# A two-layer block with a temporal conditioner: another order of the pieces on every engine, one of seven trace sums on VectorE, output rows normalised by ScalarE

## The reference, cut to what matters

```python
ctx = causal_ema(x, tau_ctx)                                    # a scan over the 512 tokens
wg = sigmoid(concat([x, ctx]) @ Wg.T + bg);  gated = x * wg
h1 = gelu(x @ Wn1.T + bn1);  mod = 0.5 + sigmoid(h1 @ Wn2.T + bn2)      # 8 values per token
traces = [causal_ema(gated * mod[:, d:d+1], tau[d]) for d in range(8)]
temporal = sum_d(softmax(blend)[d] * traces[d])
gate = sigmoid(temporal @ Wtemp.T + btemp)
soma = gelu(x @ Wsoma.T + bsoma)
out = (soma * gate) @ Wout.T
z = (out - mean(out)) / sqrt(var(out) + 1e-5) * gamma + beta
# then: router logits of z, the 8 largest of 64, their softmax weights; a shared expert on z;
# the 64 routed experts; x = x + routed + shared
```

## Time and profile before

| | before |
|---|---|
| median of 3 runs | 1252.2 us (1246.92 to 1252.47) |
| profiled execution: time, span | 1251.99 us, 1250.2 us |
| PE busy | 976.5 us (78%) |
| DVE busy | 742.4 us (59%) |
| POOL busy | 665.0 us (53%) |
| ACT busy | 455.0 us (36%) |
| mean granted TensorE clock | 0.880 of full speed |

### The profile page before, as it was taken

How to read it: one execution, slowest core, us unless ns; L and a number is a source line. 1 busy time by engine, 2 the same in 40 slices (tenths; PEclk the granted TensorE clock), 3 DMA queues, 4 the chain that set the end, 5 groups by cost and what they waited for, 6 DMA issues and landing times.

```text
span 1250.2 us, 15128 instructions
## 1 busy us (share of the span) xinstructions
PE 976.5 (78%) x4616; PEld 698.3 (56%) x4616; DVE 742.4 (59%) x1547; ACT 455.0 (36%) x811; POOL 665.0 (53%) x474
## 2 busy tenths in 40 slices
PE   5894079999999999875657778678657698888880
PEld 3673069998998999842224344344344365555550
DVE  1444656666665766416566666767774677666730
ACT  1221144635546445424343544444421032222230
POOL 1110224545535545238787586776872167777771
PEclk9765579999999999886878888898878799999995
DMA  2355714444444333232112231321311689998967
GB/s 65 114 164 186 270 44 104 87 92 109 88 113 84 88 72 52 51 101 76 44 68 73 88 118 56 105 89 69 124 55 39 225 212 250 257 253 242 259 105 147
DMA packets 90450, 151.22 MB, mean 121 GB/s; under 512 B 15816, under 2 KB 72848, under 8 KB 87248
## 3 DMA queue, kind: packets, MB, share of 16 engines
q1 hardware_dynamic: 55184, 95.46, 23.4%
q0 software_dynamic: 25104, 39.86, 17.4%
q10 hardware_dynamic: 10096, 15.10, 3.6%
HBM read 115.37 MB, written 43.42 MB: 127 GB/s over the span
## 4 chain that ended last, share of the span: by engine, by line
PE 47%; POOL 12%; issue 10%; DVE 10%; DMA 8%; POOLq 4%; DVEq 3%; ACT 2%; ACTq 0%
PE bank L1497 14%; PE bank L1482 13%; DMA out<-ys,slots 5%; POOL acc L604 5%; PE bank L1509 5%; PE bank L1598 4%; POOLq L603 3%; DMA odd_rows<-ys,slots 2%; POOL xg L650 2%; DVE body L1150 2%; POOL odd_rows L657 2%; POOL out L657 2%; PE bank L1404 2%; PE bank L1581 2%; PE bank L1467 1%
## 5 line engine op out<-in xcount | busy, mean ns | idle before, releaser
L801 ACT ACTIVATE h_raw<-bank,b 128x512 f32<-128x512 f32 x128 | 88.1, 688 | 168.8 <-PE bank L1482 166.5
L1150 DVE TENSOR_TENSOR_SCAN body<-bank,body 128x512 f32<-128x512 f32 x112 | 129.7, 1207 | 30.1 <-POOL acc L604 27.2
L1497 PE MATMUL bank<-w_hi,h_hi 128*128 128x256 f32 x512 | 144.6, 282 | 0.1
L1105 DVE TENSOR_TENSOR h_lo<-h_raw,h_hi 128x512 fp32r<-128x512 f32 x128 | 87.2, 692 | 94.3 <-ACT h_hi L805 94.3
L1497 PE MATMUL bank<-w_lo,h_hi 128*128 128x256 f32 x512 | 142.4, 278 | 0.0
L1497 PE MATMUL bank<-w_hi,h_lo 128*128 128x256 f32 x512 | 142.3, 278 | 0.0
L604 POOL TENSOR_TENSOR acc<-acc,body 128x1024 f32<-128x1024 f32 x56 | 132.3, 2363 | 12.8 <-issue 11.0
L578 POOL DMA_INDIRECT x_rows<-ob,put x64 | 110.5, 1727 | 27.7 <-issue 14.6
L1482 PE MATMUL bank<-ex_hi,w_hi 128*128 128x512 f32 x256 | 100.6, 393 | 4.9 <-issue 4.9
L1482 PE MATMUL bank<-ex_hi,w_lo 128*128 128x512 f32 x256 | 101.6, 397 | 0.0
L1482 PE MATMUL bank<-ex_lo,w_hi 128*128 128x512 f32 x256 | 101.2, 395 | 0.0
(11 more groups left out here) (229 smaller groups left out, 2191.0 us busy)
## 6 DMA issues: line engine op xcount, KB each, us to landing
body<-in_mwp SPq DMA_DIRECT2D x46, 512.0 KB, 4.4
head<-in_mwp SPq DMA_DIRECT2D x18, 512.0 KB
w1s<-in_fW SPq DMA_DIRECT2D x8, 1024.0 KB, 4.8
w2s<-in_fW SPq DMA_DIRECT2D x8, 1024.0 KB, 5.3
md<-m_rows SPq DMA_DIRECT2D x8, 1024.0 KB, 4.8
body<-m_rows SPq DMA_DIRECT2D x8, 1024.0 KB, 5.6
z_rows<-zrow SPq DMA_DIRECT2D x8, 640.0 KB, 3.2
xt<-in_x SPq DMA_DIRECT2D x8, 512.0 KB
```

The costliest lines, as they stand in the source:

```text
L801: A.activation(h1_raw[f % 4][:, :], bank[:, 2 + f % 4, :], ACT.Gelu_apprx_tanh, bias=b1_0[:, bass.ds(e, 1), f]).then_inc(b_h, 1)
L1105: V.tensor_tensor(h1_lo[:, f, :], h1_raw[f % 4][:, :], h1_hi[:, f, :].bitcast(F32), ALU.subtract).then_inc(b_lo, 1)
L1150: o = V.tensor_tensor_scan(dst[:, c, :], decay[:, d:d + 1].to_broadcast([P, S]), drive[(D * b + d) % DRIVES][:, c, :], 0.0, ALU.mult, ALU.add)
L1497: o = T.matmul(rows4(6)[:, j, :], x[:, f, rows], w[q][:, f * H:(f + 1) * H], start=(f == 0 and n == 0), stop=(f == FT0 - 1 and n == 2))
```

## The change

Every engine gets a new order of the same pieces, with loops over b written out. POOL, DVE and ACT of step b become (PE and SP in the diff):

- POOL: rstd_of(b-2), drive(b-1,7), add(b-1,5), drive(b,0), drive(b,1), add(b-1,6), add(b-1,7), drive(b,2), add(b,1), drive(b,3), drive(b,4), add(b,2), add(b,3), drive(b,5), drive(b,6).
- DVE: scan 0, scan 1, shared_b(b-2), ctx_scan(b+1), pick(b-2), scan 2, gate_soma(b-1), scan 3, shared_a(b-2), route_weights(b-2), scan 4, stats(b-1), add(b,4), scan 5, gate_in(b+1), scan 6, finish(b-2), scan 7.
- ACT: z_out(b-2), soma_out(b), weighted(b,2), x1T_out(b+1), shared_b_out(b-2), weighted(b,3), h1_out(b+1), gate_out(b-1), weighted(b,4), weighted(b,5), shared_out(b-2), exponentials(b-2), weighted(b,6), t8_out(b+1), weighted(b,7), wg_out(b+1), normalise(b-1), weighted(b+1,0), weighted(b+1,1).

The sum of trace 4 is made by DVE, the other six stay on POOL. The rows are normalised by ACT as rstd times out plus a shift, and POOL's `rstd_of` makes that shift with two more instructions of 128x4. The steps run from b = -1, and the last share from b = B + 1.

```diff
             def rstd_of(q):
                 pool.wait_ge(c_mv, level(q))
                 pool.wait_ge(c_no, level(q - 1))
-                settle(pool, tally)
                 G.tensor_scalar(veps1[:, :], mv1[:, :, 1], 4 * EPS, None, ALU.add)
+                G.tensor_scalar(shift1[:, :], mv1[:, :, 0], -1.0, None, ALU.mult)
                 pool.drain()
-                G.tensor_tensor(rstd1[:, :], veps1[:, :], mhalf[:, :], ALU.pow).then_inc(c_rs, 1)
+                G.tensor_tensor(rstd1[:, :], veps1[:, :], mhalf[:, :], ALU.pow)
+                pool.drain()
+                G.tensor_tensor(shift1[:, :], shift1[:, :], rstd1[:, :], ALU.mult).then_inc(c_rs, 1)
...
+            def normalise(q):                                  # ACT
+                act.wait_ge(c_rs, level(q))
+                act.wait_ge(c_zst, level(q - 1, 16))
+                act.wait_ge(c_zm, level(q - 1))
+                for j in range(TT):
+                    o = A.activation(zrow[:, j, 0:H], rows4(0)[:, j, :], ACT.Identity, bias=shift1[:, j:j + 1],
+                                     scale=rstd1[:, j:j + 1])
+                o.then_inc(c_no, 1)
...
+            def add_trace(b, d):                               # DVE
+                dve.wait_ge(c_scan, level(D * b + d))
+                if d > 1:
+                    dve.wait_ge(c_add, added(b, d - 1))
+                dve.drain()
+                V.tensor_tensor(acc[b % 2][:, :, :], acc[b % 2][:, :, :], trace[((D - 1) * b + d - 1) % TRACES], ALU.add).then_inc(c_add, 1)
...
             def route_weights(q):
                 dve.wait_ge(c_ex, level(q))
+                dve.wait_ge(c_zst, level(q - 1, 16))
...
             # SP, step b
-                if share:
-                    q = b - 2
-                    sp.wait_ge(c_fin, level(q - 1))
-                    sp.dma_start(xr[:, :, :], ...).then_inc(c_xr, 16)
-                    sp.wait_ge(c_zr, level(q))
-                    sp.dma_start(z_rows[...], zrow[:, :, :]).then_inc(c_zst, 16)
-                if front:
-                    m_load(b + 1, 0)
-                if share:
-                    sp.wait_ge(c_fin, level(q))
-                    sp.dma_start(out[...], ost[:, :, :]).then_inc(c_ost, 16)
-                if front:
-                    m_load(b + 1, 1)
+                if on(b - 2):
+                    row_in(b - 2)
                 if b == B:
                     sp.wait_ge(c_add, added(B - 1, D - 1))
                     for e in range(HEADS, RING):
                         e_load(e)
+                if ahead(b + 1):
+                    m_load(b + 1, 0)
+                if on(b - 2):
+                    z_store(b - 2)
+                if ahead(b + 1):
+                    m_load(b + 1, 1)
+                if on(b - 2):
+                    row_store(b - 2)
...
             # PE, step b
-                for d in range(D):
-                    if d == 0 and front:
-                        h1_in(b + 1)
-                    if d == 1 and share:
-                        shared_a_in(b - 2)
-                    if d == 1 and gate:
-                        temp_in(b - 1, 1 - p, front)
-                    if d == 2 and front:
-                        t8_in(b + 1)
-                    if d == 3 and gate:
-                        out_in(b - 1)
-                    if d == 3 and front:
-                        wg_in(b + 1, 0)
-                    if d == 4 and front:
-                        wg_in(b + 1, 1)
-                    if d == 4 and share:
-                        down_in(b - 2, gate, front)
-                    if d == 6 and front:
-                        soma_in(b + 1)
-                    if d == 6 and gate:
-                        z_in(b - 1)
-                    if d == 7 and gate:
-                        logits_in(b - 1)
-                    if d == 7 and load:
-                        x1T_in(b + 2, h + 1, p)
-                    if d == 7 and gate:
-                        shared_b_in(b - 1, front)
+                if ahead(b + 1):
+                    x1T_in(b + 1)
+                if on(b - 2):
+                    shared_b_in(b - 2)
+                if on(b - 2):
+                    logits_in(b - 2)
+                if ahead(b + 1):
+                    h1_in(b + 1)
+                if on(b - 1):
+                    temp_in(b - 1)
+                if on(b - 2):
+                    shared_a_in(b - 2)
+                if ahead(b + 1):
+                    t8_in(b + 1)
+                if on(b - 1):
+                    out_in(b - 1)
+                if ahead(b + 1):
+                    wg_in(b + 1)
+                if on(b - 2):
+                    down_in(b - 2)
+                if on(b - 1):
+                    z_in(b - 1)
+                if ahead(b + 1):
+                    soma_in(b + 1)
```

More of the change, by code:

```diff
@@ L350, in ffn, with on, ahead, conditioning @@
             group(E0 // 2 - 1, True)
[L352 to L358, removed]
+        def on(n):
+            return 0 <= n < B
+        def ahead(n):
+            return 0 < n < B
         def added(b, d):
             return level((D - 1) * b + d - 1)
-        def conditioning(eng, first, step):
+        def conditioning(first, step):
             first()
[L370 to L378, removed]
+            for b in range(-1, B + 2):
+                step(b)
         @block.sync
@@ L616, in _, with step @@
             ffn(pool, b_group)
-            def step(h, p, load, front, middle, gate, share):
-                b = 2 * h + p
-                for d in range(D):
[L621 to L633, removed]
+            def step(b):
+                if on(b - 2):
+                    rstd_of(b - 2)
+                if on(b - 1):
+                    drive_of(b - 1, 7)
+                if on(b - 1):
+                    add_trace(b - 1, 5)
+                if on(b):
+                    drive_of(b, 0)
+                if on(b):
+                    drive_of(b, 1)
+                if on(b - 1):
+                    add_trace(b - 1, 6)
+                if on(b - 1):
+                    add_trace(b - 1, 7)
+                if on(b):
+                    drive_of(b, 2)
+                if on(b):
+                    add_trace(b, 1)
+                if on(b):
+                    drive_of(b, 3)
+                if on(b):
+                    drive_of(b, 4)
+                if on(b):
+                    add_trace(b, 2)
+                if on(b):
+                    add_trace(b, 3)
+                if on(b):
+                    drive_of(b, 5)
+                if on(b):
+                    drive_of(b, 6)
+                if b == B:
+                    pool.wait_ge(c_som, level(B - 1))
+                    pool.drain()
+                    for r in range(RING):
+                        o = G.memset(wdb[r][0:P - FR, :], 0.0)
+                    o.then_inc(e_pad, 1)
@@ L917, in front_only @@
                 h1_out(0)
-                t8_out(0, 0)
+                t8_out(0)
                 wg_out(0)
-                soma_out(0, 0)
-                weighted(0, 0, 0)
-                weighted(0, 0, 1)
-                x1T_out(1)
-            conditioning(act, front_only, step)
+                soma_out(0)
+            conditioning(front_only, step)
             def silu(e):
@@ L1301, in last_share, with step @@
                 dve.drain()
-            def step(h, p, load, front, middle, gate, share):
-                b = 2 * h + p
-                if isinstance(b, int) and b == B + 1:
+            def step(b):
+                if b == B + 1:
                     dve.drain()
@@ L1687, in row_0 @@
                     t8_in(0)
[L1688 to L1689 removed]
+                    wg_in(0)
                 else:
```

269 lines of the change are left out of this document (152 added, 117 removed).

## The result

The changed kernel takes 1166.3 us (median of 4 runs, 1161.8 to 1167.2); the kernel before took 1251.7 beside it. The ratio is 0.932, with a 95% interval of 0.928 to 0.935. The forecast was 1176, with 1159 to 1204 as its range. The profiled execution took 1165.94 us, its span 1164.2.

A forecast was written before the change was run, and what follows sets the result against it. A ring of waits, not work, was taken to set the 50.9 us step. Five new steps of 39.5, limited by DVE (34.6 + 4.7), with first steps and tail, gain 76 us: span 1174.2 plus 1.8 is 1176 us, range 1159 to 1204.

The forecast's parts named there:

- What bounds it: Conditioning's 50.9 us middle step: a ring of waits; an older sequence's share delays the gate, blocking ACT, starving POOL 14.5 us.
- The step, 39.5: A middle conditioning step in the new order takes 39.5 us, with DVE as its limit; five such steps.
- the step is shorter than I think: Rival: DVE's waits come out smaller, POOL's 37.1 us limits the step, 12 us less, 1164; chance 0.12.
- the term of DVE: DVE per step: 34.6 us of work plus 4.7 for four waits on POOL (bounds 0 and 9.4), 39.3.
- The lock's price on POOL: POOL, held up by DVE instructions with two SBUF inputs, pays 1.1 us for the sum, 0.2 for each other.
- The first two steps: From drive(0,0) at 558.5, drive(1,0) comes at 589 and drive(2,0) at 626.5 us.
- `normalise` on ACT: ACT normalises the rows in four PSUM reads of 0.38, 1.5 us a step, covered by 2 us of slack.
- The tail: After the last sum: normalise(7) starts 20 us behind it instead of 20.8, then 24.7 us unchanged to the first gather.
- Tripping: Rival: nearly full POOL and DVE wait for each other, step 44 us, total 1200; chance 0.24, store's landings included.
- The wait of `normalise` for the store: Rival: z_store(b-2), behind m_load, lands late, 3 us a step, 15 us, 1191; counted within tripping's 0.24.
- PE at its lower clock: Rival: PE's matmuls run mostly at 1.2 GHz, PE needs 54.7 us a step, eating the gain; all low 1321; chance 0.05.
- Changes nothing: Rival: in the new order the ring through gate_out only closes elsewhere, 1252; chance 0.04.

The follow-up runs named there:

- order_only_early: Changed kernel with trace 4's sum back on POOL and normalise back on DVE, between scan 5 and gate_in, with the old rstd_of: 1179.7 us, ratio 0.944.
- normalise_on_dve_early: Changed kernel with normalise back on DVE, between scan 5 and gate_in, and the old rstd_of: 1177.5 us, ratio 0.940.
- pow_only_store_first: Changed kernel with rstd_of's two small preparations made by DVE behind stats, and z_store issued ahead of the experts' weights: 1165.3 us, ratio 0.932.
- more_dve: Changed kernel with one more 128x512 scan on DVE in each step, into a tile nothing reads: 1163.4 us, ratio 0.931.
- normalise_on_dve: Changed kernel with normalise back on DVE, between finish and the last scan, and the old rstd_of: 1193.3 us, ratio 0.955.
- moves_only: Kernel before, in its old order, with trace 4's sum moved to DVE and normalise to ACT: 1256.6 us, ratio 1.006.
- sum4_on_pool: Changed kernel with trace 4's sum put back on POOL, behind drive(b,6): 1177.1 us, ratio 0.944.

## Why the prediction was right, point by point

**What bounds it: half right.** That waits and not work set the step, that POOL starves for `gb`, and that the new order frees it, the changed kernel and order_only_early show. That one link, the share ahead of the gate, is the cause, they don't: exchanging that pair alone gave 0.4%, and 48.7 of POOL's 52.3 us of waits stayed. The prediction read the ring's last wait and took it for the whole ring; with the pair exchanged `temp_in` waits for the last sum instead, and the share's output on ACT still stands between the gate and `weighted`. It forecast the changed kernel rightly because the new order opens all links at once, and because the step was laid out engine by engine and not got by taking one wait off. Which exchanges of the new order are needed wasn't tried one by one, and stays open.

**The step, 39.5: the mis-sized term; 37.15 measured.** Over five steps 189.0 us instead of 197.5 (the first of them took 40.4), 8.5 less. POOL's 37.1 was right to a tenth, and it is the limit, as the rival "the step is shorter than I think" had it (1164; measured 1166.3). So the likeliest case, DVE as the limit and 1168 to 1188, did not come, and a rival with a chance of 0.12 did. What failed is the term of DVE: four lock waits, taken at half a POOL instruction each, 4.7 in all. They measured 2.7 in the middle steps: cast 1.17, product with `ex` 0.07, product with `wsum` 1.33, sum 0.10. Of the 39.3 another 1.2 were too much in the work itself (36.1 busy). The size wasn't wrong everywhere: 4.4 in the changed kernel's first full step, in normalise_on_dve_early and in pow_only_store_first, whose steps took 40.4, 40.4 and 38.8. That four of the five steps fell into the pattern with 2.7 was luck that no sum of average waits could tell; and more_dve shows that on the engine with slack the waits shrink as work is added.

**The lock's price on POOL: right.** 1.1 was taken for the sum, and `veps` paid 0.97; of the 0.2 for each of the others, drives of 2.53 and 2.70 instead of 2.35 show it. The Trainium skill, SBUF — State Buffer, section Who interferes with whom, has the lock as exclusive and in both directions; the trace agrees (0.23 to 1.20 on POOL, 0.72 to 2.75 on DVE's cast).

**The first two steps: 71.1 instead of 68**, 3.1 too little, nearly all of it in the first (33.5 instead of 30.5): POOL stood 3.5 us ahead of its first sum and four drives took 2.9 to 3.3 us. **drive(7,0) to the end of the last sum: 42.3 instead of 42.1.**

**`normalise` on ACT: mis-sized, at no cost.** It was taken at 1.5 from four reads of 0.38; with scale and bias per partition it takes 1.93. It costs nothing, since the cover that was named held; ACT is busy for 23.9 of 37.15.

**The tail: the store's wait right, the rest mis-sized by 2.9.** The experts' weights do stand ahead of `z_store(6)`:

```profile
858.21 0.34 SPq L418 DMA_DIRECT2D body<-in_mwp  x1
...
870.43 0.38 SPq L442 DMA_DIRECT2D z_rows<-zrow  x1
```

Its landing took 6.2 us, to 876.6, and `normalise(7)` started then, though `shift_b` had stood at 874.2:

```profile
876.76 1.93 ACT L897 ACTIVATE zrow<-bank,shift_b,rstd_b 128x256 f32<-128x256 f32 x4 [9.16 <-issue]
```

That is 18.6 us behind the last sum, where 20 was forecast. But from there to the first gather (904.38) it took 27.6 us and not 24.7, "nothing changes". The same matmuls were slower, after PE had stood 5.2 us for the rows:

```profile
878.74 1.88 PE L1635 MATMUL bank<-ident,zrow 128*128 128x128 f32 x8 [5.17 <-ACT zrow L897]
882.16 3.68 PE L1642 MATMUL bank<-router,zT 128*128 128x64 f32 x16 [1.54 <-ACT zT L905]
...
891.47 5.40 PE L1660 MATMUL bank<-zT,ws_gu 128*128 128x512 f32 x8 [1.52 <-DVE hsB L1271]
```

In the kernel before they took 1.10, 3.20 and 3.70 there, 3.0 us less. In pow_only_store_first the store's wait was gone (`normalise(7)` at 874.09, released by POOL), and the last of them took 5.40 all the same. So the wait for the store is not the cause of the lower clock by itself; what is wasn't tried.

**The rivals.** "Tripping" didn't come: no step reached 44. The wait of `normalise` for the store came in small. In four middle steps the store landed after 7.4 to 7.5 us, near the longest of the earlier trace rows, and that landing, 0.4 us after `shift_b` in three of them and 1.4 in the fourth, was what released `normalise`, which started 0.1 us or less behind it. That is inside the cover: POOL's drives behind it came on time. The profile puts three of these waits down to `shift_b` (above). PE at its lower clock didn't come either: the clock rose to 1.00 and 0.97 as PE's gaps closed. It was the right danger, though: in normalise_on_dve, where PE stands 6.6 us for the rows, eight matmuls then take 5.7 us instead of 3.7. "Changes nothing" came for the exchange of one pair and for the two moves in the old order, and not for the new order.

In sum: forecast 1176, measured 1166.3. Of the span's difference (1174.2 to 1164.2), the five steps give 8.5, the microsecond for joints wasn't needed, and work that isn't touched gives 2.8 ahead of the phase and 2.8 behind it; the first two steps take 3.1 back, and the tail 1.5 (46.2 instead of 44.7). The 5.6 us of work that isn't touched belong to no term of the forecast: without them it would have been 1172, and the range would have held as well. The 8.5 too much for the steps and the 4.6 too little for the first two steps and the tail partly cancelled, which is luck too.

## What to carry to other kernels

When in-order queues wait for each other in a ring, don't price a change by the one wait that ended last: lay the whole new step out by engine. Here POOL's sum was right to 0.1 us, while exchanging the worst link alone gave 0.4%. Work moved between two nearly full engines paid only once the ring was open. And time that an engine waits inside its instructions for another is no work: carry it as a range, forecast the step for both of its ends, and expect a small edit to move it from one to the other (2.7 and 4.4 us a step here).

## What the runs showed of the hardware

- DVE's 128x256 f32 product of two SBUF tiles took 0.42 to 2.23 us beside a running POOL (longest in moves_only), and its cast to bf16, which has one input, 0.72 to 2.97 (longest in order_only_early); a tiny POOL instruction (128x4) took 1.20 instead of 0.23 under DVE's sum. The profile books all of this as busy time.
- Two gaps of 2.0 us on PE at the same place of two steps (pow_only_store_first) had different ends: 16 matmuls at a granted clock of 0.50 in 3.51 us, and the same at 1.00 in 1.89.
- An ACT read of 128x256 from PSUM with scale and bias per partition took 0.56 us, without them 0.38.
- The windows' busy time per step is a reading with an edge: in sum4_on_pool DVE shows 36.3 us in a step of 38.7 and 34.7 in one of 39.7, by where the windows cut its stream.
